# One region of rows per expert, and the tile list cut at the full tiles of three images instead of at two images

## What is computed

```
logits = x @ Wr + br                          # 8 experts, the best 2 of each token
w      = softmax over the two chosen logits
h      = gelu(layernorm_e(x) @ W1[e] + b1[e]) # 128 -> 512
y      = h @ W2[e] + b2[e]                    # 512 -> 128
out    = x + sum over the two experts of w * y
```

## Time and profile before

| | us |
|---|---|
| median of the three runs | 734.39 (730.04 to 734.54) |
| the profiled execution | 726.86 |
| its span, first to last instruction | 725.0 |
| PE busy in the span | 652.2 (90%) |
| ACT, DVE, POOL busy | 440.7, 430.7, 235.6 |

### The profile page before, as it was taken

The page is one execution under the profiler, slowest core; times in us unless marked ns, Lnnn a source line. Parts: engine busy times, 40 slices in busy tenths (PEclk is TensorE's granted clock), DMA queues, the critical chain, the costliest instruction groups (busy, mean ns, idle before and its releaser), DMA issues.

```text
span 725.0 us, 16938 instructions
## 1 busy us (share of the span) xinstructions
PE 652.2 (90%) x5378; PEld 495.2 (68%) x5378; DVE 430.7 (59%) x1375; ACT 440.7 (61%) x1283; POOL 235.6 (32%) x348
## 2 busy tenths in 40 slices
PE   2997999999899999988998998976889999999982
PEld 2695567666557767655785755654458999999981
DVE  5207847553994764398477628868555754465442
ACT  1307843653983365488535647824687789999951
POOL 4200014200201474020146502014433677754450
PEclk9999999999999999999999999988699999999995
DMA  8300000000100001000000154001310534364215
GB/s 291 142 0 31 1 1 6 2 0 19 41 2 1 6 28 34 2 29 2 1 6 20 37 186 111 1 2 34 83 38 5 155 86 102 105 196 121 64 39 181
DMA packets 36354, 40.04 MB, mean 55 GB/s; under 512 B 12176, under 2 KB 27936, under 8 KB 35980
## 3 DMA queue, kind: packets, MB, share of 16 engines
q1 hardware_dynamic: 30412, 27.47, 13.0%
q0 software_dynamic: 4704, 9.40, 4.0%
q10 hardware_dynamic: 1152, 2.10, 0.8%
HBM read 25.64 MB, written 15.17 MB: 56 GB/s over the span
## 4 chain that ended last, share of the span: by engine, by line
PE 69%; DVE 14%; ACT 10%; issue 3%; DMA 2%; POOL 1%; POOLq 0%; SPq 0%; DVEq 0%; ACTq 0%
PE ps L2212 9%; PE ps L2230 9%; PE ps L1826 8%; PE ps L1751 7%; PE ps L1811 6%; PE ps L1868 6%; PE ps L1756 4%; PE ps L1898 4%; ACT r_P L954 3%; DVE nmx L1272 3%; PE ps L1971 2%; PE ps L1928 2%; PE ps L1913 1%; ACT r_vw L903 1%; PE ps L1798 1%
## 5 line engine op out<-in xcount | busy, mean ns | idle before, releaser
L954 ACT ACTIVATE r_P<-ps,nmx 128x225 f32<-128x225 f32 (+1 forms) x192 | 85.9, 469 | 57.0 <-DVE nmx L1272 56.9
L1272 DVE TENSOR_REDUCE nmx<-ps 128x4 f32<-128x900 f32 (+1 forms) x64 | 73.7, 1157 | 22.3 <-PE ps L1868 21.4
L713 POOL TENSOR_TENSOR rstd<-vpe,minus_half 128x8 f32<-128x8 f32 x8 | 13.3, 1660 | 199.1 <-DVE vpe L1209 199.1
L791 POOL DMA_INDIRECT xs_d<-pay,pos x64 | 62.3, 974 | 34.9 <-DVE nmx L1272 19.9
L765 POOL TENSOR_TENSOR r_gh<-r_gh,nmw 113x392 f32<-113x392 f32 (+1 forms) x20 | 15.6, 781 | 137.3 <-DVE nmw L1311 137.2
L1826 PEld LDWEIGHTS ps<-r_vc,w_sb 128*128 128x128 f32 x256 | 46.2, 188 | 19.3 <-issue 15.9
L1826 PE MATMUL ps<-r_vc,w_sb 128*128 128x225 f32 x256 | 58.8, 375 | 0.0
L1751 PE MATMUL ps<-ident,r_P 128*128 128x128 f32 (+1 forms) x384 | 53.1, 279 | 6.4 <-ACT R L967 2.5
L1811 PE MATMUL ps<-r_kc,w_sb 128*128 128x225 f32 x256 | 58.2, 375 | 0.0
L1751 PEld LDWEIGHTS ps<-ident,r_P 128*128 128x128 f32 (+1 forms) x384 | 45.1, 149 | 17.8 <-issue 8.2
L2212 PE MATMUL ps<-xwin,wx_room 128*128 128x128 f32 x416 | 55.1, 276 | 0.0
(11 more groups left out here) (248 smaller groups left out, 1469.6 us busy)
## 6 DMA issues: line engine op xcount, KB each, us to landing
xrow_room<-xs_d SPq DMA_DIRECT2D x40, 65.0 KB, 1.9
qwT<-xs_d SPq DMA_DIRECT2D x38, 65.0 KB, 1.9
x_sb<-x SPq DMA_DIRECT2D x4, 512.0 KB, 3.6
w_sb<-w1k SPq DMA_DIRECT2D x1, 2048.0 KB, 7.9
w_sb<-w1v SPq DMA_DIRECT2D x1, 2048.0 KB, 12.4
w_sb<-fw SPq DMA_DIRECT2D x1, 2048.0 KB, 8.5
w_sb<-fw SPq DMA_DIRECT2D x4, 512.0 KB, 9.4
r_vw<-z_d SPq DMA_DIRECT2D x8, 256.0 KB, 3.6
```

What stands on the lines that cost most here:

```text
L791: gp.indirect_dma_start(xs_d, bass.IndirectOffsetOnAxis(pos[:, NT * k + t:NT * k + t + 1], 0), pay[:, k, t, :], None).then_inc(scattered, 16)
L954: last = sc.activation(Pb[t % NRING][:, h, 0:m], bank(name)[:, (h % 2) * m:(h % 2) * m + m], ACT.Exp, bias=nmx[:, t % NRING, h:h + 1], acc ...
L1272: ve.tensor_reduce(nmx[:, t % NRING, :].rearrange("p (a h) -> p a h", a=2), v.rearrange("p a (h m) -> p a h m", h=2), AX.X, ALU.max, negat ...
```

## The change

There is now one region per expert for the rows of all four images (`CAP`), and one running count of picks, which is no longer cleared between batches. The list is still made in two parts, but cut elsewhere. The first has the first 41 full tiles of images 0 to 2 (`NFULL`: 6144 picks are 48 tiles, less seven that may be partly filled), the second the 30 that are left, those of image 3 among them; 71 in all, NSTEP = 76. Full tiles need no padding, so only the second list has pads, issued behind row loads 32 to 39.

The first list now needs image 2's ranks, and is made in image 3's selected stage, steps 0 to 4. Its rows need image 2's scatters; POOL issues these without the pace, while images 0 and 1 keep it. `rows_written(0)` waits for the scatters of three images and for no pads.

The second list has more parts (what each expert has left before and after image 3, with jumps over what the first list took); it is made in steps 16 to 20, and PE turns it in step 21 instead of 20. Adding up over the experts is done by doubling (3 or 4 operations) in place of 7 single adds. The tables' scratch lies in the tile `hk`, which is free by then.

The loads for images 0 and 1's sums stand behind the last row load (tile 70). Their sums are in steps 65 to 71 (`NDONE` = 55, and 10 or 13), PE's transposes in 68, 70, 71 and 73.

The core of the diff (left out: index edits that follow from one region, and the plan of the PSUM banks, in which the first table's bank is 6 instead of 7):

```diff
-SPLIT = 2
-BATCH = [list(range(SPLIT)), list(range(SPLIT, B))]
-CAP = [len(g) * N + 128 for g in BATCH]
-NTILE = [2 * len(g) * N // 128 + E - 1 for g in BATCH]
+SPLIT = 3
+EARLY, LATE = (0, 1), (2, 3)
+CAP = B * N + 128
+NFULL = 2 * SPLIT * N // 128 - (E - 1)
+NDONE = 2 * SPLIT * N // 128 + E - 1
+NTILE = [NFULL, 2 * B * N // 128 + E - 1 - NFULL]
...
-REGION = [E * c + NPAD * 128 for c in CAP]
-ORIGIN = [0, REGION[0]]
+REGION = [E * CAP + NPAD * 128]
...
-TSTEP = 24
+TSTEP = B * N // 128
...
-PAD_AT = 31
+PAD_AT = 32
...
-STEP_TT, STEP_RT, STEP_RK, STEP_TAB = STEP_OS + 6, STEP_OS + 7, STEP_OS + 10, STEP_OS + 16
-TAB_SLOT = 0 if SPLIT == B - 1 else 2
-TAB_BANK = 6 if SPLIT == B - 1 else 7
-
-
-def sums_load(b):
-
-    return NTILE[0] + XRING + (-1, 2, 7)[b]
+STEP_TT, STEP_RT, STEP_RK, STEP_TAB = STEP_OS + 6, STEP_OS + 7, STEP_OS + 10, STEP_OS + 17
+TAB_AT = 3
...
-    return NTILE[0] + (9, 13, 18)[b]
+    return NDONE + (10, 13)[b]
...
+ROW_FULL = ROW_BR + E
+ROW_NEXT = ROW_FULL + TSTEP
+ROW_JUMP = ROW_NEXT + 2 * E
+NROW = ROW_JUMP + 2 * E
...
             def rows_written(q):
 
-                sp.wait_ge(pad_in, 16 * (2 + E * (q + 1)))
-                sp.wait_ge(scattered, 16 * 2 * NT * (BATCH[q][-1] + 1))
+                if q:
+                    sp.wait_ge(pad_in, 16 * (1 + E))
+                sp.wait_ge(scattered, 16 * 2 * NT * (B if q else SPLIT))
...
-            for e in range(E):
-                tail_pad(0, e)
...
-                for b in BATCH[0]:
-                    if n == sums_load(b):
-                        load_sums(b)
-            for b in BATCH[1]:
+            for b in range(B):
...
-                    pool.wait_ge(max_ready, (b + 1) * 2 * NT + NT + i + 1)
+                    if b + 1 < SPLIT:
+                        pool.wait_ge(max_ready, (b + 1) * 2 * NT + NT + i + 1)
...
+            for k in range(3):
+                ve.memset(run[k][:, :], 0.0)
+            ve.memset(marks[:, :], 0.0)
...
                     if b == SPLIT:
-                        if t == TAB_SLOT:
-                            tails_and_tiles(0)
-                        if t == TAB_SLOT + 2:
-                            tiles_up_to(0)
-                        if t == TAB_SLOT + 4:
-                            table_columns(0)
-                        if t == TAB_SLOT + 7:
+                        if t == 0:
+                            full_tiles()
+                        if t == 1:
+                            running_sums(3)
+                            first_list()
+                        if t == 2:
+                            taken_tiles()
+                        if t == 3:
+                            tiles_with_rows(0)
+                        if t == TAB_AT + 1:
                             table_rows(0)
...
-            def tails_and_tiles(q):
-
-                base = ROW_BASE1 if q else ROW_BASE
-                step(ve.tensor_tensor(tailf[:, :], cnt[0:1, q, :], rows[0:1, base:base + E], ALU.add))
-                ve.tensor_copy(tail_i[:, q, :], tailf[:, :]).then_inc(tail_ready, 1)
+            ends = marks[:, E:3 * E + 2].rearrange("p (q e) -> p q e", q=2)[:, :, 0:E]
+
+            def tails():
+
+                step(ve.tensor_tensor(tailf[:, :], cnt[0:1, 1, :], rows[0:1, ROW_BASE:ROW_BASE + E], ALU.add))
+                ve.tensor_copy(tail_i[:, :], tailf[:, :]).then_inc(tail_ready, 1)
+
+            def over(q, at_):
+
                 step(ve.tensor_tensor(steps[:, :, :], cnt[:, q, :].unsqueeze(2).to_broadcast([128, E, TSTEP]),
-                                      rows[:, ROW_STEP:ROW_STEP + TSTEP].unsqueeze(1).to_broadcast([128, E, TSTEP]), ALU.is_gt))
-                step(ve.tensor_reduce(ntl[:, :], steps[:, :, :], AX.X, ALU.add))
-                step(ve.tensor_copy(upto[:, 0:1], ntl[:, 0:1]))
-
-            def tiles_up_to(q):
-                for e in range(1, E):
-                    step(ve.tensor_tensor(upto[:, e:e + 1], upto[:, e - 1:e], ntl[:, e:e + 1], ALU.add))
-
-            def table_columns(q):
+                                      rows[:, at_:at_ + TSTEP].unsqueeze(1).to_broadcast([128, E, TSTEP]), ALU.is_gt))
+
+            def full_tiles():
+                over(0, ROW_FULL)
+                step(ve.tensor_reduce(run[0][:, E:2 * E], steps[:, :, :], AX.X, ALU.add))
+
+            def tiles_with_rows(q):
+                over(q, ROW_STEP)
+                step(ve.tensor_reduce(ends[:, q, :], steps[:, :, :], AX.X, ALU.add))
+
+            def running_sums(stages):
+
+                n = 2 ** stages
+                for i, (k0, k1) in enumerate(((0, 1), (1, 2), (2, 1), (1, 2))[0:stages]):
+                    src, dst = run[k0], run[k1]
+                    step(ve.tensor_tensor(dst[:, E:E + n], src[:, E:E + n], src[:, E - 2 ** i:E - 2 ** i + n], ALU.add))
+
+            def list_columns(q, first_row):
 
                 m = NTILE[q]
-                first = col("j128b", 0, m) if q else col("j128", 0, m)
-                step(ve.tensor_scalar(past[0:m, 0, :], upto[0:m, :], col("j", 0, m), None, ALU.is_le))
-                step(ve.tensor_scalar(past[0:m, 1, :], ntl[0:m, :], -128.0, float(CAP[q]), ALU.mult, ALU.add))
-                step(ve.tensor_tensor(past[0:m, 1, :], past[0:m, 1, :], past[0:m, 0, :], ALU.mult))
-                step(ve.tensor_reduce(tabf[0:m, :], past[0:m, :, :], AX.X, ALU.add))
                 if q:
                     dve.wait_ge(*filled("tb0"))
                 ve.tensor_scalar(tab[0:m, 0:1], tabf[0:m, 0:1], float(E - 1), None, ALU.min)
-                ve.tensor_tensor(tab[0:m, 1:2], tabf[0:m, 1:2], first, ALU.add).then_inc(tab_columns, 1)
+                ve.tensor_tensor(tab[0:m, 1:2], first_row, col("j128", 0, m), ALU.add).then_inc(tab_columns, 1)
+
+            def first_list():
+
+                m = NTILE[0]
+                step(ve.tensor_scalar(past[0:m, 0, 0:E], run[1][0:m, E:2 * E], col("j", 0, m), None, ALU.is_le))
+                step(ve.tensor_scalar(past[0:m, 1, 0:E], run[0][0:m, E:2 * E], -128.0, float(CAP), ALU.mult, ALU.add))
+                step(ve.tensor_tensor(past[0:m, 1, 0:E], past[0:m, 1, 0:E], past[0:m, 0, 0:E], ALU.mult))
+                step(ve.tensor_reduce(tabf[0:m, :], past[0:m, 0:2, 0:E], AX.X, ALU.add))
...
+            def taken_tiles():
+
+                step(ve.tensor_scalar(taken[:, :], run[1][:, E - 1:2 * E], float(NFULL), None, ALU.min))
+                step(ve.tensor_tensor(marks[:, 0:E], taken[:, 1:E + 1], taken[:, 0:E], ALU.subtract))
+
+            def second_list_parts():
+
+                step(ve.tensor_tensor(run[0][:, E:3 * E].rearrange("p (q e) -> p q e", q=2), ends,
+                                      marks[:, 0:2 * E].rearrange("p (q e) -> p q e", q=2), ALU.subtract))
+                step(ve.tensor_tensor(jump[:, :].rearrange("p (q e) -> p q e", q=2),
+                                      marks[:, 1:2 * E + 1].rearrange("p (q e) -> p q e", q=2), ends, ALU.subtract))
+                step(ve.scalar_tensor_tensor(out=jump[:, :], in0=jump[:, :], scalar=128.0,
+                                             in1=rows[:, ROW_JUMP:ROW_JUMP + 2 * E], op0=ALU.mult, op1=ALU.add))
+
+            def second_list():
+
+                m = NTILE[1]
+                step(ve.tensor_scalar(past[0:m, 0, :], run[2][0:m, E:3 * E], col("j", 0, m), None, ALU.is_le))
+                ve.tensor_tensor(past[0:m, 1, :], past[0:m, 0, :], rows[0:m, ROW_NEXT:ROW_NEXT + 2 * E], ALU.mult)
+                step(ve.tensor_tensor(past[0:m, 2, :], past[0:m, 0, :], jump[0:m, :], ALU.mult))
+                step(ve.tensor_reduce(tabf[0:m, :], past[0:m, 1:3, :], AX.X, ALU.add))
+                step(ve.scalar_tensor_tensor(out=tabf[0:m, 1:2], in0=marks[0:m, 0:1], scalar=128.0,
+                                             in1=tabf[0:m, 1:2], op0=ALU.mult, op1=ALU.add))
+                list_columns(1, tabf[0:m, 1:2])
...
+                    if k == STEP_RK + 2:
+                        tails()
                     if k == STEP_RK + 3:
-                        tails_and_tiles(1)
+                        tiles_with_rows(1)
                     if k == STEP_RK + 4:
-                        tiles_up_to(1)
+                        second_list_parts()
                     if k == STEP_RK + 5:
-                        table_columns(1)
+                        running_sums(4)
+                    if k == STEP_RK + 6:
+                        second_list()
...
-                for i in BATCH[1]:
+                for i in LATE:
...
-                    if t == TAB_SLOT + 6 and b == SPLIT:
+                    if t == TAB_AT and b == SPLIT:
```

More of the change, by code:

```diff
@@ L245, in psum_plan @@
         late(*expert_names(k))
-        for i in BATCH[0]:
+        for i in EARLY:
             late(*(f"out{j}@{i}" for j in out_half(k, i)))
-    for i in BATCH[1]:
+    for i in LATE:
         late(f"out0@{i}", f"out1@{i}")
@@ L425, in build @@
         b2_all = x_sb[:, :]
-        steps = sb("steps", [128, E, TSTEP])
+        hk_flat = hk[:, :, :].rearrange("p a m -> p (a m)")
```

(22 more changed lines are left out.)

37 lines of the change are left out of this document (14 added, 23 removed).

## The result

| | before | after |
|---|---|---|
| median of the timed runs, us | 732.83 (730.04 to 734.54, 4 runs) | 713.02 (711.07 to 713.92, 4 runs) |
| profiled execution, us (span) | 726.86 (725.0) | 713.71 (711.7) |
| ratio of the times | | 0.9734 (95% interval 0.9698 to 0.977) |

The change saves 2.7%, which is 19.5 us by the ratio. The forecast was 720.1 us with a range of 714.5 to 725.5: the sign is right, and the kernel is 7 us faster than forecast and 1.5 us under the range.

What follows compares the result with a forecast made beforehand. PE was taken to bound the expert phase; -13.3 - 0.85 + 0.2 - 0.1 - 0.4 + 0.1 = -14.3 us, from a median of 734.4 to 720.1 us, range 714.5 to 725.5.

Steps and rivals of the forecast that it cites:

- Part 1: Expert phase: 71 steps' tiles instead of 78, seven fewer at 1.896 us each, -13.3 us.
- Part 2: Second list's table: PE's wait for it falls from 1.25 to about 0.4 us, -0.85 us.
- Part 3: First list's table, moved into image 3's selected stage: DVE work mostly hidden, +0.2 us; two matmuls leave image 2's stage, -0.1.
- the ring: Image 3's selected stage: scores (PE), maxima (DVE), exponentials (ACT), no engine full; its gaps were to hide the first table.
- Part 4: Image 2's scatters, unpaced, must land before the first row load: cost 0, slack 1.8 us.
- rival D: Image 2's scatters stretched beside DVE's work; at three times their length the kernel is 14.3 us slower, 748.7; chance 0.03.
- Part 5: Where the two lists meet: tile 41's row arrives before PE takes it, cost 0, slack 3.4 us.
- Part 6: First sums, issued behind the last row load: 0 us, bound +1; the last turned half hidden, -0.4 us.
- The turned half: Last of four output halves turned by PE, falling where POOL sends its final scatters: hidden, -0.4 us.
- Part 7: Start: PE's first matmul waits for constants whose rows grow from 93.5 to 125.5 KB, +0.1 us.

Runs made afterwards that it cites:

- tiles78: The changed kernel with seven more empty tiles in the second list and the sums moved to match: 725.9 us, ratio 0.9949.
- after_c: The changed kernel run again with no edit, for one more profile: 712.06 us in its one run.
- after_again: The changed kernel run once more with no edit: 711.25 us beside 729.29 of the kernel before, ratio 0.9759.
- sums2_late: The changed kernel with the loads for image 2's sums waiting again for all 71 tiles instead of the first 55: 716.18 us, ratio 0.9838.
- unpaced_before: The kernel before, with image 2's scatters no longer waiting for image 3's maxima: 732.04 us beside 731.38, ratio 1.0018.

## Why the prediction was right and wrong, point by point

**Part 1, seven steps: right.** Steps of 1.896 us before and after, and tiles78 gives 13.28 us for seven.

**Part 2, the second table: right.** -0.85 forecast; the wait fell from 1.25 to 0.49, -0.76. The steps 17 to 20 ran as worked out: DVE was ahead of PE in each until the list itself. The wait repeats: 1.25 to 1.31 us in the four profiles of before, 0.48 or 0.49 in the three of after.

**Part 3, the first table in the ring: right, once the clock is told apart.** Read plainly, the two first profiles say +1.27 (24.03 for 22.76), six times the forecast. But the ring's length goes with the instant at which the granted clock comes back: among the five executions without the new table it is 22.76 at 6.5 us, 23.68 at 8.5, 23.70 at 8.6, 24.15 at 9.6 and 24.17 at 9.8, about 0.4 us for each us of delay. On that line (its ends are the first and the last of the five) 9.1 us gives 23.87, where after and after_c have 24.03; 9.9 gives 24.21, and after_again has that; 7.0 gives 22.97, where sums2_late has 23.06; 6.8 gives 22.89, where tiles78 has 22.97. The table costs the ring 0 to 0.16 us, with the five themselves up to 0.07 off the line. In all thirteen profiles the clock had fallen to 0.50 at least 6.6 us ahead of the first maxima. Why it came back early in some executions and late in others isn't settled: sums2_late and after_again run the same code up to there, and differ by 2.9 us.

**Part 4, the scatters: right.** Cost 0. Spacing 19.10/15 = 1.27 (1.26 forecast), load 3.39 us behind the last scatter (3.2 forecast), row there at 533.61 + 1.9 = 535.5, and taken at 538.48: the slack is 3.0, where 1.8 was forecast, since the ring was longer. The longest of the sixteen took 1.10 us on POOL, and in after they landed 2.3 us behind their issue, one of them 3.3. No scatter in after or unpaced_before, with DVE more than half busy beside them, took above 1.10, so rival D has nothing for it. The Trainium skill's page "SBUF — State Buffer", section "SBUF: two separate sides", gives 3100 ns for a DMA issued by GpSimd that overlaps a VectorE `tensor_copy`, and names the copy from SBUF to SBUF in FP32 as one that takes the shared ports. All copies that DVE made beside these sixteen (`R<-ps`, and in after `tab_i<-ps`) read PSUM, so the runs don't test that case and say nothing against the page. What they show is that its figure does not apply to this mix of operations.

**Part 5, the lists' edge: right.** Tile 41's row was loaded at 624.29 and taken at 629.70. Counted from the first row transpose (538.48) that is 85.8 and 91.2 us; the forecast's 620.5 and 625.8, counted from the 534.74 of before, are 85.8 and 91.1. PE never waits there.

**Part 6, the sums: the step that failed.** It priced the sums of images 0 and 1 and ended with "hidden, **-0.4**". What the prediction says of image 2 is one sentence ahead of the parts, "Behind 708 us comes the tail: the last scatter landing, the sums of images 2 and 3, four stores", and from there on the tail is taken as it was. That took a term of the sum for nothing, without a reason. The load of an image's sums waits for the tiles of the first part or for all of them, and the part of the diff shown further up leaves out the lines that say which:

```diff
-                q = 0 if b < SPLIT else 1
-                for n in range(NTILE[0] + q * NTILE[1] - XRING, NTILE[0] + q * NTILE[1]):
+                done = NDONE if b < SPLIT else NALL
+                for n in range(done - XRING, done):
```

SPLIT went from 2 to 3. With all rows of the first three images in the first 55 tiles (`NDONE`), image 2 no longer waits for the last one. What its loads wait for now is the buffer, which image 0's sums must leave: PE turns image 0's second half at 686.12, and the loads start at 686.84. So image 2's share of the tail runs beside PE's last steps and image 3's scatters. That is a term of -3.0 us in the tail (17.0 to 14.0 in the means, 17.3 to 14.0 in the two first profiles) that the sum doesn't have; sums2_late puts it back, 14.1 to 17.3.

The turned half was priced at -0.4 and gave about -0.3. The last of the four stands at 692.35, right ahead of the last two groups of PE's L2269. From the last L2251 to the last scatter it is 6.49 us in before and 6.64 in sums2_late, which has the turned half there but not image 2's work. With image 2's loads and sums beside them it is 7.16 in after and 6.90 in after_again, and in after the last two scatters take 1.45 and 1.02 us (0.96 and 0.96 in before and in sums2_late). So image 2's work gives some 0.4 us back ahead of the last scatter; the cause of the longer scatters is not shown.

**Part 7, the start: too small to tell.** PE's first matmul went from 5.81 to 6.08 in the first profiles, but it stands at 5.74 to 6.69 in the five profiles with before's start and at 5.82 to 6.39 in the eight with after's. The means differ by the +0.1 forecast, and the ranges overlap.

**The sum against the time.** The stretches that repeat give (159.08 - 173.02) + (14.00 - 17.00) = -16.9 us, as means over the three and the four profiles of the unchanged kernels, and the ring +0.1: **-16.8**. The forecast had -14.4 there. The difference is the tail's 3.0, less the 0.6 by which the stretch to the last scatter, at -13.9, falls short of its -14.5 (parts 1, 2 and 6). The timed ratios of this kernel, 0.9734 and 0.9759, are -19.5 and -17.6 us, with intervals of -22.1 to -16.9 and -20.0 to -15.2: -16.8 is at the edge of the first and inside the second. What may lie between them is ahead of image 3's first maxima, which come at 515.5 in the mean of the five kernels with before's tables (511.98 to 518.38) and at 512.8 in that of the eight with after's (511.13 to 514.45). Half of those 2.7 us arise ahead of image 1's selected stage, where the change alters only the start (32 KB more of constants, one store of padding less, four small memsets), and the ranges overlap, so the profiles don't settle it. The timed runs say that it is more than scatter: the 41 of before have a mean of 731.0 us and the 9 of after one of 712.1, 18.9 apart with about 1.1 to either side. Some 2 us thus lie outside the stretches that I can account for, and no experiment here shows what they are.

**The level.** Of the 7.1 us between 720.1 and 713.0, 1.6 are the reference: the three runs shown had a median of 734.39, and the medians of before in the comparisons since were 732.83, 729.29, 731.38 and 731.42. Another 2.4 are the step that failed, as the stretches show it. The last 3.1 are open, and with them the cause of a good part of the miss: neither the missing term alone nor the term with the reference would have put the time under the 714.5 of the range.

## What to carry to other kernels

When a constant changes, look up every condition that it stands in, the waits of the last stage above all: here one comparison with SPLIT moved 3 us of work off the tail, and the part of the diff that I took for the core left its lines out. Price the tail by its own chain of waits, transfer by transfer, even where the change seems to end ahead of it. And before a difference of a microsecond between two profiles is put down to a change, compare several profiles of the same kernel stretch by stretch, with the granted clock beside each.

## What the hardware showed that I had not expected

The same kernel's spans differed by 6.9 us (725.0 to 731.9) with nothing changed. A part of it goes with TensorE's granted clock in stretches where PE is partly idle: at 1.00 or 0.66 in 60 to 70 us, and, in the last ring, back from 0.50 (1.2 GHz) to 1.00 (2.4 GHz) between 6.5 and 9.9 us behind the same instruction. With each us of delay the ring was 0.4 us longer. In the expert phase, at 1.00 throughout, the stretch of 173 us repeats within 0.12 us over five executions.
